# Router loop unrolled with its sum on ScalarE, shared experts reordered, and expert rows gathered two blocks ahead

## The reference, cut to what matters

```python
xn = (x - mean(x)) / sqrt(var(x) + 1e-5)            # per token, D = 512
affinity = sigmoid(xn @ wa)                         # 16 routed experts
best two experts of each token, their affinities divided by their sum
expert(v) = (gelu(v @ g + gb) * (v @ w1 + b1)) @ w2 + b2   # 512 -> 256 -> 512
out = x + xn + sum of 2 shared experts(xn)
            + sum over the token's two experts of share * expert(xn)
```

## Time and profile before

| | us |
|---|---|
| median of 3 runs (1394.67 to 1398.93) | 1395.43 |
| the profiled execution | 1397.62 |
| its span in the profile | 1395.8 |
| router stage | 885.5 to 945.4 |
| routing tables and shared experts | 945.4 to 1115.3 |
| routed experts | 1115.3 to 1358.7 |
| combine | 1358.7 to 1395.8 |

### The profile page before, as it was taken

How to read it: one execution, slowest core, us unless ns; L and a number is a source line. 1 busy time by engine, 2 the same in 40 slices (tenths; PEclk the granted TensorE clock), 3 DMA queues, 4 the chain that set the end, 5 groups by cost and what they waited for, 6 DMA issues and landing times. The chain is left out here.

```text
span 1395.8 us, 25868 instructions
## 1 busy us (share of the span) xinstructions
PE 1098.3 (79%) x9603; PEld 808.6 (58%) x9603; DVE 937.3 (67%) x1668; ACT 710.0 (51%) x1077; POOL 634.1 (45%) x589
## 2 busy tenths in 40 slices
PE   5899987289994998368888887777799598999950
PEld 4677766145541666146666665576477287788740
DVE  6489998678885575477777777697545355455526
ACT  4466736278882554246666666362344134444420
POOL 1344434245552222167776677341682234455520
PEclk9999998689997999759999999558899789999985
DMA  6664411013333132201111110572587548777749
GB/s 245 193 222 130 142 38 39 30 61 120 121 121 123 38 105 76 74 25 47 46 47 47 47 47 2 191 265 94 142 218 248 165 141 250 253 257 237 232 140 351
DMA packets 79289, 187.34 MB, mean 134 GB/s; under 512 B 10303, under 2 KB 12501, under 8 KB 78281
## 3 DMA queue, kind: packets, MB, share of 16 engines
q1 hardware_dynamic: 60040, 137.03, 30.6%
q0 software_dynamic: 8544, 24.68, 5.6%
q10 hardware_dynamic: 10592, 24.12, 5.3%
HBM read 131.37 MB, written 48.14 MB: 129 GB/s over the span
## 5 line engine op out<-in xcount | busy, mean ns | idle before, releaser
L376 PE MATMUL ps_y<-kv,toep 128*128 128x288 f32 x640 | 159.6, 412 | 7.2 <-DMA toep<-taps_padded 7.0
L376 PEld LDWEIGHTS ps_y<-kv,toep 128*128 128x128 f32 x640 | 123.0, 193 | 43.2 <-DMA toep<-taps_padded 8.6
L1376 POOL TENSOR_TENSOR at_pl<-at_pf,at_ph 128x1024 bf16<-128x1024 f32 x64 | 136.5, 2133 | 0.7 <-ACT at_ph L1426 0.7
L2202 POOL DMA_INDIRECT expert_results<-sgu,target x47 | 69.2, 1473 | 97.3 <-ACT sgu L2230 97.3
L360 POOL TENSOR_TENSOR kv<-kx 128x1024 f32<-128x1024 f32 x32 | 60.6, 1894 | 88.8 <-PE ps_y L376 39.3
L1422 ACT ACTIVATE at_pf<-ps_st 128x1024 f32<-128x1024 f32 x64 | 65.3, 1020 | 57.7 <-PE ps_st L1551 54.4
L1467 DVE TENSOR_REDUCE at_negmax<-ps_s 128x4 f32<-128x1024 f32 x64 | 78.2, 1222 | 14.4 <-PE ps_s L1515 12.9
L893 PEld LDWEIGHTS ps_eg<-e_xT,e_w 128*128 128x128 bf16 x1128 | 68.7, 100 | 11.9 <-issue 1.5
L893 PE MATMUL ps_eg<-e_xT,e_w 128*128 128x128 bf16 x1128 | 72.6, 222 | 0.7 <-ACT e_xT L2246 0.7
L2271 DVE COPY e_w<-expert_weights 128x4096 bf16 x47 | 57.7, 1227 | 22.9 <-issue 22.9
L2246 ACT ACTIVATE e_xT<-ps_ex 128x512 bf16<-128x512 bf16 x47 | 28.1, 597 | 87.7 <-PE ps_ex L2320 87.7
(11 more groups left out here) (382 smaller groups left out, 3228.4 us busy)
## 6 DMA issues: line engine op xcount, KB each, us to landing
sgu<-down_parts SPq DMA_DIRECT2D x47, 512.0 KB, 4.5
w_raw<-in_L_ffn_w ACTq DMA_DIRECT2D x32, 512.0 KB, 4.4
toep<-taps_padded SPq DMA_DIRECT2D x32, 256.0 KB, 3.6
f_draw<-in_L_ffn_rw SPq DMA_DIRECT2D x16, 512.0 KB, 4.2
down_parts<-f_dparts SPq DMA_DIRECT2D x16, 512.0 KB, 2.9
s_raw<-in_L_ffn_rg SPq DMA_DIRECT2D x16, 512.0 KB, 4.7
s_raw<-in_L_ffn_rw SPq DMA_DIRECT2D x16, 512.0 KB, 5.0
m_got<-expert_results SPq DMA_DIRECT2D x16, 512.0 KB, 10.1
```

The source lines that it names most:

```text
L376: last = pe.matmul(y[:, l * B:(l + 1) * B, :, WIDE - 1:], toep[h % 2][:, (DC - 1 - l + m) * P:(DC - l + m) * P], kv[h % 2][:, m * B:(m + 1 ...
L1376: pool.tensor_tensor(pl[u % 4][:, :, :, :], pf[u % 2][:, :, :, :], ph[u % 4][:, :, :, :], ALU.subtract) .then_inc(p_low, 1)
L2202: pool.indirect_dma_start(out=k.scratch["results"], out_offset=bass.IndirectOffsetOnAxis(ap=target[:, j:j + 1], axis=0), in_=yo[j % 2], in ...
```

## The change

**Router.** The loops are written out, with static addresses. The power of the variance is made for 4 columns and then for 12. The sum of residual and xn goes from GpSimd to ScalarE, as x * (1 + rstd) - mean * rstd, with `gain` and `shift` made by VectorE. psX has four buffers; the high and the low part of the turned tile are made from PSUM and not from xT. The weights' high parts are made by GpSimd, and their low parts by VectorE within the loop, after tiles 5, 7, ... 15.

**Shared experts.** `cols` lies in the buffers of x; all three raw buffers are loaded at once, x after the turn. The shares come ahead of hidden(0, 0) on VectorE, are turned behind up(0, 1) and kept in chunk 0. TensorE's order becomes up(i, 0), down(i - 1), up(i, 1), and `down` does both tiles for expert 0, then for expert 1. VectorE's order becomes gate(i, 0), up_lows, low_part(i, 0), add_sums(i - 1), gate(i, 1), up_lows, low_part(i, 1). The last chunk's x lies in two buffers of the next stage, and the end of the stage no longer waits for the last stores; the next stage does, on SP and ahead of ScalarE's first two outputs.

**Routed experts.** Turn n gathers block n + 2 instead of n + 1; the bias products stand behind up(0).

```diff
@@ router
-        psX = [ctx.enter_context(nc.psum_tensor(f"ps_rx{i}", [P, D], F32)) for i in range(2)]
+        psX = [ctx.enter_context(nc.psum_tensor(f"ps_rx{i}", [P, D], F32)) for i in range(SETS)]
...
         @block.gpsimd
-            pool.tensor_tensor(rstd[:, :], var[:, :], k.pow_half[:, :], ALU.pow).then_inc(rstd_ready, 1)
-                    pool.tensor_tensor(row(k.x, t), row(k.x, t), xn[p][:, :].unsqueeze(1), ALU.add).then_inc(added, 1)
+            for tiles in (slice(0, FRONT), slice(FRONT, NT)):
+                pool.tensor_tensor(rstd[:, tiles], var[:, tiles], k.pow_half[:, tiles], ALU.pow).then_inc(rstd_ready, 1)
+            for n in range(6):
+                pool.wait_ge(w_loaded[n], 16)
+                pool.tensor_copy(place(n, 0), raw[n][:, :]).then_inc(w_high, 1)
...
         @block.vector
-                dve.tensor_tensor(turned[q][:, 1, :, :], xT[p][:, :, :], turned[q][:, 0, :, :], ALU.subtract).then_inc(x_low, 1)
+                dve.tensor_tensor(turned[q][:, 1, :, :], chunks(psX[q][:, :]), turned[q][:, 0, :, :], ALU.subtract).then_inc(x_low, 1)
+            def weight_lows(n):
+                dve.wait_ge(w_high, n + 1)
+                dve.tensor_tensor(place(n, 1), raw[n][:, :], place(n, 0), ALU.subtract)
...
+            scales(1, slice(0, FRONT))
+            normalise(0)
+            normalise(1)
+            for t in range(NT):
+                split(t)
+                if t + 2 < NT:
+                    normalise(t + 2)
+                if t == 0:
+                    scales(2, slice(FRONT, NT))
+                if t >= 5 and t % 2:
+                    weight_lows((t - 5) // 2)
...
         @block.scalar
+                act.activation(xT[t % 2][:, :, :], chunks(psX[q][:, :]), ACT.Copy).then_inc(xT_ready, 1)
+                if t >= SETS:
+                    act.wait_ge(turned_stored[q], 16 * (t // SETS))
+                act.activation(turned[q][:, 0, :, :], chunks(psX[q][:, :]), ACT.Copy).then_inc(x_high, 1)
+                if t in (0, FRONT):
+                    act.wait_ge(scaled, 2 if t == 0 else 4)
+                act.activation(k.x[:, t, :], k.x[:, t, :], ACT.Identity, bias=shift[:, t:t + 1], scale=gain[:, t:t + 1]).then_inc(added, 1)
@@ shared experts, SP
-            for n in range(RAW_N - 1):
+            for n in range(RAW_N):
                 load_raw(n)
...
+            sp.wait_ge(cols_turned, 2)
             for s in range(ST):
                 load_x(0, s)
-            sp.wait_ge(cols_turned, 2)
-            load_raw(RAW_N - 1)
...
-                for n in range(i * PER + RAW_N, min((i + 1) * PER + RAW_N, 2 * E_N)):
+                for n in range(RAW_N + max(i * PER - 1, 0), min((i + 1) * PER - 1 + RAW_N, 2 * E_N)):
                     load_raw(n)
             for s in range(ST):
                 store_x(CH - 2, s)
+            sp.wait_ge(gu_psum, CH * SH_N)
+            for s in range(ST):
                 load_x(CH - 1, s)
...
             for s in range(ST):
+                sp.wait_ge(x_stored[s], 16 * (CH - 1))
+            for s in range(ST):
                 store_x(CH - 1, s)
-            for s in range(ST):
-                sp.wait_ge(x_stored[s], 16 * CH)
@@ shared experts, VectorE's chunk loop
-                hidden(i, 0)
+                gate(i, 0)
+                if i > 1:
+                    up_lows(2 * i - 1)
+                low_part(i, 0)
+                add_sums(i - 1)
+                gate(i, 1)
                 up_lows(2 * i)
-                hidden(i, 1)
-                add_sums(i - 1)
-                up_lows(2 * i + 1)
+                low_part(i, 1)
@@ shared experts, ScalarE
-                    if i == 1 and e == 0:
+                    if i == 0 and e == 1:
                         keep_shares()
@@ shared experts, TensorE
             up(0, 0, 1)
+            turn_shares()
             for i in range(1, CH):
...
-                for e in range(SH_N):
-                    pe.wait_ge(y_full, i * SH_N + (e - 1))
-                    up(i, i % 2, e)
-                    if i == 1 and e == 0:
-                        turn_shares()
+                pe.wait_ge(y_full, i * SH_N - 1)
+                up(i, i % 2, 0)
                 down(i - 1)
...
+                pe.wait_ge(y_full, i * SH_N)
+                up(i, i % 2, 1)
             down(CH - 1)
@@ routed experts
-                if 2 <= n + 1 < NBLK:
-                    gather(n + 1)
+                if n + 2 < NBLK:
+                    gather(n + 2)
...
+                else:
+                    act.wait_ge(x_stored[j], 16 * CH)
...
                 if n < NBLK:
                     up(n)
+                if n == 0:
+                    block_biases()
```

More of the change, by code:

```diff
@@ L1631 @@
 HI_AT = 64
+FRONT = 4
 K_ROWS = 96
@@ L1643, in stage_router @@
         wa = sb("r_wa", [P, DC, E_N], F32)
-        mean, var, tmp, rstd = (sb(f"r_{n}", [P, NT], F32) for n in ("mean", "var", "tmp", "rstd"))
+        mean, var, tmp, rstd, gain, shift = (sb(f"r_{n}", [P, NT], F32) for n in ("mean", "var", "tmp", "rstd", "gain", "shift"))
         xn, xT = two("r_xn", [P, D], F32), two("r_xT", [P, DC, P], F32)
@@ L1714, in _, with scales @@
             dve.sem_inc(var_ready, 1)
-            dve.wait_ge(rstd_ready, 1)
-            def normalise(t, p):
-                if not known(t) or t >= 2:
-                    dve.wait_ge(rows_low, t - 1)
-                    dve.wait_ge(added, t - 1)
-                    dve.wait_ge(x_psum, t - 1)
-                scale = (mean[:, bass.ds(t, 1)], rstd[:, bass.ds(t, 1)], ALU.subtract, ALU.mult)
-                dve.tensor_scalar(xn[p][:, :], row(k.x, t), *scale).then_inc(xn_ready, 1)
-            def split(t, p, q):
+            def scales(n, tiles):
+                dve.wait_ge(rstd_ready, n)
+                dve.tensor_scalar(gain[:, tiles], rstd[:, tiles], 1.0, None, ALU.add).then_inc(scaled, 1)
+                dve.scalar_tensor_tensor(shift[:, tiles], mean[:, tiles], -1.0, rstd[:, tiles], ALU.mult, ALU.mult).then_inc(scaled, 1)
@@ L1726, in split, with normalise @@
+            def normalise(t):
+                if t >= 2:
+                    dve.wait_ge(x_psum, t - 1)
+                    dve.wait_ge(rows_low, t - 1)
+                dve.tensor_scalar(xn[t % 2][:, :], k.x[:, t, :], mean[:, t:t + 1], rstd[:, t:t + 1], ALU.subtract, ALU.mult).then_inc(xn_ready, 1)
+            def split(t):
+                q = t % SETS
                 dve.wait_ge(rows_high, t + 1)
-                dve.tensor_tensor(rows[q][:, 1, :], xn[p][:, :], rows[q][:, 0, :], ALU.subtract).then_inc(rows_low, 1)
+                dve.tensor_tensor(rows[q][:, 1, :], xn[t % 2][:, :], rows[q][:, 0, :], ALU.subtract).then_inc(rows_low, 1)
@@ L1747, in _, with turn @@
             dve.tensor_tensor(down_bias[lows, :], bias_raw[lows, :], down_bias[lows, :], ALU.subtract)
-            for n in range(6):
-                dve.wait_ge(w_high, n + 1)
-                dve.tensor_tensor(place(n, 1), raw[n][:, :], place(n, 0), ALU.subtract)
         @block.tensor
         def _(pe):
-            def turn(t, p):
+            def turn(t):
                 pe.wait_ge(xn_ready, t + 1)
-                if not known(t) or t >= 2:
-                    pe.wait_ge(xT_ready, t - 1)
+                if t >= SETS:
+                    pe.wait_ge(x_low, t - SETS + 1)
@@ L1767, in score @@
                 last.then_inc(logits, 1)
             pe.wait_ge(wa_loaded, 16)
-            turn(0, 0)
-            turn(1, 1)
-            with pe.Fori(0, NT // 2 - 1) as i:
-                for p in range(2):
-                    score(i * 2 + p, p)
-                    turn(i * 2 + (p + 2), p)
-            for t in range(NT - 2, NT):
-                score(t, t % 2)
+            turn(0)
+            turn(1)
+            for t in range(NT):
+                score(t)
+                if t + 2 < NT:
+                    turn(t + 2)
@@ L1799, in _, with stage_route_and_shared @@
             act.activation(down_bias[:, :], bias_raw[:, :], ACT.Copy).then_inc(bias_high, 1)
-            for n in range(6):
-                act.wait_ge(w_loaded[n], 16)
-                act.activation(place(n, 0), raw[n][:, :], ACT.Copy).then_inc(w_high, 1)
-def stage_route_and_shared(k, xaff, sgu, sd, down_bias, xT, W, bias_rows, expert, token, target, weight, e_rows, e_parts, fetched):
+def stage_route_and_shared(k, xaff, sgu, sd, down_bias, xT, W, bias_rows, expert, token, target, weight, e_rows, e_parts, e_yo, fetched):
     nc = k.nc
@@ L1834, in stage_route_and_shared @@
         warm = sb("s_warm", [P, 1], F32)
-        x = [sb(f"s_x{i}", [P, D], F32) for i in range(ST)]
+        x = sb("s_x", [P, ST, D], F32)
         gf = two("s_gf", [P, F2, CHUNK], F32)
@@ L1959, in _, with gate @@
             link = Link(dve, dve_step)
-            def hidden(i, e):
+            def gate(i, e):
                 dve.wait_ge(gelu_done, i * SH_N + (e + 1))
@@ L2009, in _ @@
             dve.wait_ge(dve_step, link.at())
+            hidden(0, 0)
             dve.wait_ge(counted, 1)
```

(2 more changed lines are left out.)

127 lines of the change are left out of this document (53 added, 74 removed).

## The result

The changed kernel takes 1359.66 us, the median of four runs, of which three lie between 1357.12 and 1361.41 us (median 1357.92) and one, at 2136 us, was a disturbed execution and is left out of the ratio. Against the kernel before (1397.18 us, median of four runs) the ratio is 0.9718, 95% interval 0.9670 to 0.9767: about 39 us faster. Forecast was 1344.2 us, a ratio of 0.9633. The profiled execution took 1357.12 us with a span of 1355.4 us, 40.4 us less than the span before.

The account below looks back on a forecast made before the run. TensorE and VectorE were taken as full in the router, TensorE as the shared loop's floor, with routed experts waiting for gathered rows; 9.7 + 26.5 + 2 + 13 = 51.2 us gave 1344.2 us, own range 1336 to 1353.

Parts of the forecast that it names:

- rival (b): Shared experts' loop: the conversion chain bounds it, 2 to 4 us a chunk, 14 to 28 us; 1353 to 1367 us, chance 0.20.
- Its idle time in the loop, 44.1 less 42.33, is all there is: Router loop: TensorE's busy time was taken as the floor, so the loop could gain only 1.8 us.
- ScalarE's sum: Router loop: a fourth ScalarE pass per tile, priced at 0.596 us by the nearest row and hidden by TensorE.
- The tail: Router, behind the last tile: six weight splits move into the loop; gain 7.0 us, bounds 5 and 7.
- Rival (a): Router: it gets the full clock and ScalarE bounds the loop at 38 us; 4.2 us better, 1340 us, chance 0.08.
- The stop: Shared experts' start: TensorE's 14.81 us idle before the first down product goes whole, plus 2.07 us of slow clock.
- The allowance of 5 us: Shared experts' loop: stalls taken over seven chunks because the slack drops to 8.0 us; bounds 0 and 25.
- rival (e): Shared experts: TensorE waits for the whole conversion chain each chunk, 76 us instead of 5; 1415 us, slower than before, chance 0.03.
- Rivals (c): Routed experts: the gathers pay nothing because the DMA engines are the limit; 13 us less gain, 1357 us, chance 0.10.
- (d): Shared experts' start: the stop stays, something else holds the shares; 14.81 + 2.07 us less gain, 1361 us, chance 0.04.
- the 2 us allowed to the next stage: Shared experts' end: of the 9.25 us gap, sum, issue and the block's start stay, about 2 us; gain 7.2.
- 13 + 2: Routed experts: 13 us from gathers issued one block earlier, 2 us at the start from bias products behind up(0).

Follow-up runs that it names:

- the second profile: The changed kernel run once more, unaltered, with a new profile: 1363.62 us, ratio 0.9744 to the kernel before; shared experts 159.5 us.
- ScalarE's order: Changed kernel with ScalarE's high part of each chunk's second hidden half put ahead of an expert-weight conversion: 1364.86 us, ratio 0.9760 to the kernel before.
- SyncE's: Changed kernel with SyncE's store of x three raw loads earlier and two raw loads between store and reload: 1346.99 us, ratio 0.9636 to the kernel before.
- the two edits of order: Changed kernel with both SyncE's earlier store of x, loads before its reload, and ScalarE's high part ahead of the conversion: 1344.16 us, ratio 0.9616.

## Why the prediction was right, and where it was off

The time fell as forecast, but it lies 15 us above the likeliest value: outside the forecast's own 1336 to 1353 us, inside the wide range (1329 to 1367 us), and where rival (b), the conversion chain with its chance of 0.20, had put it (1353 to 1367 us). In the profiled execution, 5.3 us of that are variation ahead of the router; the edited stages gave 44.7 us of the 51.2, with 2.6 and some 0.1 us more than forecast in the router and the routed experts and 9.2 us less in the shared experts.

**Router, +2.6 us.** The front gave 1.75 us (5.39 to 3.63 us up to the first transpose; forecast 1.4). The step "Its idle time in the loop, 44.1 less 42.33, is all there is" was wrong: the loop got 3.6 us shorter. The busy sum itself shrank when the waits went. Before, a tile's eight score products hold the time from their first start, 906.92, to the next transpose at 908.75, 1.83 us; after, 1.56 us from 906.90 to 908.46. Four transposes and eight products start to start make 2.45 us, the same in every profile in which VectorE is in time. That ScalarE's sum costs 0.60 us by L1792 was wrong too: 0.82 us (L1790), hidden as forecast. The tail: 7.0 forecast, 6.9 in the traces (TensorE idle 10.45 us before the shared experts, now 3.53), 7.5 by the run with the sum on GpSimd. The casts did hold VectorE at the start (a row split took 1.52 us at 900.4), but TensorE's tiles stay at 2.45 to 2.48 us there, so they were covered. Rival (a) didn't come: the loop stays at 0.50 with its tiles back to back.

**Shared start, right in kind.** The stop went whole, and the slow down(0) with it: 16.9 us less 1.0 us that the first half loses to a slower clock (0.66 instead of 0.76; 5.28 us for the first 24 products instead of 4.36).

**Shared loop, -5 us more.** The allowance of 5 us was the mis-sized term. The waits sum to 9.6 us and down(2) ran 2.3 us longer behind its stops; the old loop had 1.6 us of waits of its own, so some 10 us net, and 7 more in the second profile. The chain was named, in the allowance and in rival (b): conversion behind load, load behind store, landing and reload. The runs show two chains where the text had one, ScalarE's order and SyncE's, each of which makes TensorE wait by itself, and both are order, not bandwidth: with the two edits of order and the same transfers the waits inside the loop are 0. Rival (b) priced it at 14 to 28 us: some 10 us in the first profile is under that, some 17 in the second within. So the forecast chose the milder of its two accounts of this chain, and the better one had 0.20. Its mechanism at full strength, rival (e), was far off. Rivals (c) and (d) didn't come: the gathers paid and the stop is gone.

**Shared end, -3 us.** The last low part cost 2.48 us, not 1.5, through GpSimd's split beside it; and the 2 us allowed to the next stage were 3.86. TensorE's new order, the last chunk's x in other buffers and the store that nobody waits for were not undone one by one.

**Routed experts, the right sum of two wrong terms.** 15.1 us against 13 + 2 is in part luck. The gathers gave 15.0 us, since the waits (12.9 us) and the slow products behind them both count. The start gave 0.1 us, not 2: the bias products take 1.08 us instead of 1.94, and the second turn comes 1.9 us earlier, but the third comes 1.8 us later behind it, because block 1's products now wait 1.66 us for their turned rows instead of 0.73, and the first 24 of them take 2.72 us instead of 1.50. With the gathers' line undone and the bias products left behind up(0) the stage is as long as before.

## What to carry to other kernels

Take an engine's floor from the distance between starts in a stretch where it never waits, not from its busy sum. Where a queue that issues in program order carries both a store with a reload behind it and other loads, place those loads between the two, and place each wait at the time at which its event comes; the same can hold for a copy on the critical path that stands behind a conversion. When two chains make the same engine wait, one alone may show nothing (ScalarE's here) or nearly everything (SyncE's): try each, and both. And check each term of a sum at its own place in the trace: a sum can be right with two of its terms wrong.

## What the runs showed of the hardware

- Two instructions on GpSimd and VectorE that meet in SBUF: the one that starts second pays. A split of 128x512 with both inputs in SBUF took 0.69 us with its start 0.17 us ahead of GpSimd's sum, and another of the same size 1.75 us with its start 0.35 us behind. GpSimd's sum took 1.65 us behind such a split, and 1.27 us with none ahead of it.
- ScalarE's pass over 128x512 f32 took 0.60 us with its input in PSUM and 0.82 us with input and output in SBUF and a scale and bias per partition. Which of the two differences counts was not tried.
- TensorE's transposes and score products in f32 stayed at the lower clock (0.50) through 40 us of tiles with the next 2.45 us behind each, busy 39.90 of 40.5 us, in every profile with the new loop.
- The next stage began 4.3 to 5.8 us behind the end of GpSimd's last instruction in twelve profiles, 5.8 us in one case where no other engine did anything in the last 3.1 us (its last stores were still on their way). What takes this time is not shown.
